# Two loops over attention heads, TensorE's and ScalarE's, written out head by head

## The chip, the cores and the metric

The kernel runs on one core of one Trainium2 chip. A core has several engines that each follow their own list of instructions: TensorE (matrix products; the profile calls it PE, and its weight loads PEld), VectorE (DVE), ScalarE (ACT), GpSimd (POOL) and SyncE (SP, which here starts the DMA transfers). They meet through semaphores: an instruction adds to a semaphore when it is done, and another engine waits until the semaphore has reached a value. The metric is the device time of one execution in microseconds (us); lower is better.

## The reference

x has 2048 tokens of 512 features. All products are wanted at about fp32 precision.

```python
x = x + 0.5 * ffn(layernorm(x))        # weights in 4-bit codes with block scales, MLP width 4096
x = x + attn(layernorm(x))
x = x + 0.5 * ffn(layernorm(x))

def attn(x):                           # 16 heads of 32 features, causal
    q, k, v = split(x @ w_qkv.T + b_qkv)
    scores = q @ k.T / sqrt(32) + causal_mask
    return (softmax(scores) @ v) @ w_out.T + b_out
```

## The kernel before

The kernel has four stages in a row, each a block in which every engine has its own program: the first feed-forward part, the projection to queries, keys and values, the attention, and the second feed-forward part. A stage begins when all engines have left the one before it.

**Feed-forward.** TensorE multiplies in groups of hidden features; after some groups written out, a loop `pe.Fori(1, NGROUP // 2 - 1)` runs two groups a round. The other engines have the same loop.

**Attention.** The 16 heads go one after the other. For a head, TensorE computes the scores twice. Once with queries as rows (`max_chunk`, L797), from which VectorE takes the row maxima (L820, L828); these become two further rows of the queries (`rows`, L808 and `store_rows`, L848 on ScalarE), so that the second scores already have the maximum taken off. That second time, keys are rows (`scores`, L1350; L1358 adds the causal mask); ScalarE takes the exponential of a tile (`exps`, L1551) into a ring of 12 tiles, and TensorE multiplies four tiles at a time with the values (`value_lane`, L1364) and with ones for the sums (`sum_lane`, L1370; GpSimd adds some tiles first, L1614). ScalarE copies a finished block of outputs from PSUM (`take_out`, L1559), four blocks to a head.

The order of work is written by hand. `head(hp, s)` works on head 3 hp + s: in each of its 40 slots it computes one tile of scores four slots ahead (`AHEAD`) and one chunk for the maxima of the head behind it. So the maxima of the next head are made during this one, and the score tiles run over the boundary between two heads: a boundary is no break in the work. Operands of a head lie in one of three buffers, `s % 3`, and so a round of three heads is the natural period. Heads 0 to 14 go through `head`; head 15 through `last_head`, between whose products the output projection starts.

Five programs hold this order. VectorE's, GpSimd's and SyncE's are Python loops (`for hp in range(...)`), so every instruction of every head stands in the program once. TensorE's (L1457) and ScalarE's (L1594) are loops of the chip: `Fori` puts the three heads of a round into the program once, `hp` is a register, and the end of a round is a branch back to its first instruction. Where a wait depends on `hp`, its value (such as `120 * hp + (SLOTS * s + u + 1)`) is worked out by the engine in a register operation ahead of the wait. There are five rounds, so four branches back; the fifth time the branch isn't taken.

Of the kernel before, what the change touches and what calls it, by code (L numbers as in the profile page):

```python
# [30 lines left out]
HEADS = 16  # L31
# [1149 lines left out]
def scaled_at(n):  # L1181
    b, k = STEPS[n]
    return QUARTERS * (SCALED.index(f"block {b}" if k == LATE_K else n) + 1)
# [71 lines left out]
def attention(nc, x, bank, o_heads, sums, inverses, w_out, b_out, heads, o):  # L1255
    with ExitStack() as ctx:
# [76 lines left out]
        def _(pe):  # L1333
# [4 lines left out]
            def scores(hp, s, u, first=False):  # L1338

                b, kt = TILES[u]  # L1340
                i = s % 3
                if u in FIRST_OF_BLOCK:
                    pe.wait_ge(heads.rows_ready, 12 * hp + (4 * s + RANK[b] + 1))
                    if s == 2 and u == 0:
                        pe.wait_ge(heads.constants_ready, 7)
                if not (first and u < SCORE_BANKS):
                    pe.wait_ge(probs_ready, 120 * hp + (SLOTS * s + u - SCORE_BANKS + 1))
                q0 = max(b * TB, kt * P)
                width = (b + 1) * TB - q0
                last = pe.matmul(score_bank_of(s, u)[:, 0:width], keys[i][0:ROWS, cols(kt, P)],  # L1350
                                 queries[i][0:ROWS, q0:q0 + width], start=True, stop=(kt < 4 * b),
                                 skip_group_check=True)
                if kt < 4 * b:
                    last.then_inc(scores_ready, 1)
# [54 lines left out]
            def head(hp, s):  # L1409
                for t in range(SLOTS):  # L1410
                    of, u = divmod(t + AHEAD, SLOTS)
                    scores(hp, s + of, u)
                    masks_of(s + of, u, False)
                    heads.max_chunk(pe, hp, s + 1, t)
                    if t in ROWS_AT:
                        heads.rows(pe, hp, s + (ROWS_AT[t] not in OWN_ROWS), ROWS_AT[t])
                    masks_of(s + of, u, True)
                    if t % BATCH == BATCH - 1:
                        meet_batch(hp, s, t // BATCH)
# [34 lines left out]

            for u in range(AHEAD):
                scores(0, 0, u, first=True)
            with pe.Fori(0, HEADS // 3) as hp:  # L1457
                for s in range(3):
                    head(hp, s)
            last_head(HEADS // 3)  # L1460
# [81 lines left out]
        @block.scalar  # L1542
        def _(act):
            def exps(hp, s, u, summed=True):
                b, kt = TILES[u]
                width = TB - max(0, kt * P - b * TB)
                i = u // BATCH - RING // BATCH
                if u % BATCH == 0 and summed and i % BATCHES in QUADS:
                    act.wait_ge(quad_steps, 54 * hp + 18 * (s + i // BATCHES + 1) + 3 * (QUADS.index(i % BATCHES) + 1))
                act.wait_ge(scores_ready, 120 * hp + (SLOTS * s + u + 1))  # L1550
                act.activation(probs[:, (SLOTS * s + u) % RING, 0:width],  # L1551
                               score_bank[(SLOTS * s + u) % SCORE_BANKS][:, 0:width],
                               ACT.Exp, scale=SM_SCALE).then_inc(probs_ready, 1)

            def take_out(hp, s, e):
                act.wait_ge(out_ready, 3 * NOUT * hp + (NOUT * s + e + 1))

                act.wait_ge(out_stored[e], 240 * hp + 80 * (s + 1))
                act.activation(heads_out[:, e, :, :], out_bank[:, 0:2 * P], ACT.Copy).then_inc(out_free, 1)  # L1559

            def take_outs(hp, s, t):
                if t in OUT_DONE:
                    take_out(hp, s, OUT_DONE.index(t))

            def head(hp, s):
                for t in range(SLOTS):
                    of, u = divmod(t + AHEAD, SLOTS)
                    exps(hp, s + of, u)
                    if t in ROWS_AT:
                        heads.store_rows(act, hp, s + (ROWS_AT[t] not in OWN_ROWS), ROWS_AT[t])  # L1570
                    if t % BATCH == BATCH - 1:
                        take_outs(hp, s, t)

            def high(n):
                act.wait_ge(o.scaled, scaled_at(n))
                act.activation(o.normed_high[:, n % UNITS, :], o.from_heads[:, n % UNITS, :], ACT.Copy)\
                   .then_inc(o.scaled_high, 1)

            def last_head(hp):
                for t in range(SLOTS):  # L1580
                    if t + AHEAD < SLOTS:
                        exps(hp, 0, t + AHEAD, summed=False)
                    if t in ROWS_AT and ROWS_AT[t] in OWN_ROWS:
                        heads.store_rows(act, hp, 0, ROWS_AT[t])
                    if t % BATCH == BATCH - 1:
                        for n in STEPS_AT.get(t // BATCH + 1, BEHIND[:3]):
                            high(n)
                        take_outs(hp, 0, t)
                for n in BEHIND[3:]:
                    high(n)  # L1590

            for u in range(AHEAD):
                exps(0, 0, u, summed=False)
            with act.Fori(0, HEADS // 3) as hp:  # L1594
                for s in range(3):
                    head(hp, s)
            act.wait_ge(o.wo_loaded, 16)
            act.activation(o.wo_high[:], o.wo[:], ACT.Copy).then_inc(o.wo_high_ready, 1)
            last_head(HEADS // 3)
# [125 lines left out]
```

## Time and profile before

| | |
|---|---|
| median of 3 runs | 2982.96 us (2982.94 to 2984.21) |
| the profiled execution's own time | 2983.2 us |
| its span, first to last instruction | 2981.4 us |
| TensorE busy | 2904.1 us, 97% of the span |
| ScalarE busy | 1052.5 us, 35% |
| granted TensorE clock, mean | 0.991 of full speed |
| attention, first score product to the last head's last copied block | 1267.55 to 1877.2 us |

Times in the profile are counted from the span's start. Busy time of an engine leaves out register operations, branches and waits. A granted clock of 1.00 is 2.4 GHz, 0.50 is 1.2 GHz.

### The profile page before, as it was taken

To read this page: it belongs to the slowest core of one execution; us is meant where nothing else is said; L and a number is where in the kernel's file an instruction comes from. 1 tells how busy PE (TensorE), PEld (TensorE's weight loads), DVE (VectorE), ACT (ScalarE), POOL (GpSimd) and SP (SyncE) were. 2 spreads that over 40 slices of the span, in tenths; PEclk is the share of its full clock that TensorE was granted. 3 is DMA by queue.
4 is the path that set the end of the run, shared out by engine and by line. 5 is a ranking of instruction groups with operands and counts; after the bars stand their busy time and mean duration, and the time that the engine had idled before them with its cause. 6 is when DMAs were issued, how large, how long until landed. Compare 5 with 4: busy or idle time off the path is not lost. (4 is left out here: it accounts for less than half of the span.)

```text
span 2981.4 us, 51041 instructions
## 1 busy us (share of the span) xinstructions
PE 2904.1 (97%) x19280; PEld 2342.2 (79%) x19280; DVE 1826.8 (61%) x3312; ACT 1052.5 (35%) x1825; POOL 1069.3 (36%) x745
## 2 busy tenths in 40 slices
PE   6999999999999999999999999899999999999999
PEld 5888888888888878777777776678888888888887
DVE  5656665565666544576777675675656665565654
ACT  4322222222222222266666664432222222222222
POOL 3322222222222224466666663342222222222221
PEclk9999999999999999999999999999999999999999
DMA  3001000000000015722322222100000000000001
GB/s 99 27 24 29 21 28 21 21 25 25 28 21 28 1 47 113 220 72 59 71 59 63 68 75 71 39 29 22 26 25 28 21 28 21 21 24 26 28 8 57
DMA packets 98586, 127.95 MB, mean 43 GB/s; under 512 B 43020, under 2 KB 51196, under 8 KB 95100
## 3 DMA queue, kind: packets, MB, share of 16 engines
q1 hardware_dynamic: 98428, 125.72, 15.3%
q8 instruction: 115, 1.88, 0.3%
q14 instruction: 43, 0.35, 0.0%
HBM read 96.34 MB, written 29.34 MB: 42 GB/s over the span
## 5 line engine op out<-in xcount | busy, mean ns | idle before, releaser
L59 PE MATMUL psum<-ffn_x_high,ffn_w_high 128*128 128x512 f32 x2048 | 801.6, 391 | 16.7 <-POOL ffn_x_low L212 9.5
L60 PE MATMUL psum<-ffn_x_low,ffn_w_high 128*128 128x512 f32 x2048 | 798.0, 390 | 0.0
L61 PE MATMUL psum<-ffn_x_high,ffn_w_low 128*128 128x512 f32 x2048 | 798.0, 390 | 0.0
L589 POOL TENSOR_TENSOR ffn_inner<-ffn_gelu,ffn_inner 128x512 fp32r<-128x512 f32 x256 | 345.6, 1350 | 1169.1 <-ACT ffn_inner L527 1169.1
L434 DVE SCALAR_TENSOR_TENSOR ffn_gelu<-ffn_gelu,psum 128x512 f32<-128x512 f32 x256 | 176.0, 687 | 604.1 <-ACT ffn_gelu L520 604.1
L59 PEld LDWEIGHTS psum<-ffn_x_high,ffn_w_high 128*128 128x128 f32 x2048 | 385.0, 188 | 105.4 <-POOL ffn_x_low L212 10.0
L61 PEld LDWEIGHTS psum<-ffn_x_high,ffn_w_low 128*128 128x128 f32 x2048 | 385.0, 188 | 80.1
L60 PEld LDWEIGHTS psum<-ffn_x_low,ffn_w_high 128*128 128x128 f32 x2048 | 385.2, 188 | 79.0
L59 PE MATMUL psum<-ffn_inner,ffn_w_high 128*128 128x512 f32 x1024 | 398.6, 389 | 0.2
L60 PE MATMUL psum<-ffn_inner,ffn_w_high 128*128 128x512 f32 x1024 | 398.4, 389 | 0.0
L61 PE MATMUL psum<-ffn_inner,ffn_w_low 128*128 128x512 f32 x1024 | 398.4, 389 | 0.0
L583 POOL TENSOR_TENSOR ffn_w_low<-ffn_weight,ffn_w_high 128x1024 fp32r<-128x1024 f32 x96 | 231.4, 2410 | 373.2 <-ACT ffn_w_high L513 373.2
L1551 ACT ACTIVATE probs<-psum 128x512 f32<-128x512 f32 (+3 forms) x640 | 297.9, 535 | 175.2 <-PE psum L1358 98.8
L520 ACT ACTIVATE ffn_gelu<-psum 128x512 f32<-128x512 f32 x256 | 153.0, 598 | 532.0 <-PE psum L61 532.0
L450 DVE SCALAR_TENSOR_TENSOR x<-psum,x 128x512 f32<-128x512 f32 x512 | 321.5, 683 | 20.5 <-PE psum L61 20.5
L820 DVE TENSOR_REDUCE chunk_max<-psum 128x1 f32<-128x512 f32 x384 | 249.6, 685 | 114.3 <-PE psum L797 114.3
L527 ACT ACTIVATE ffn_inner<-ffn_gelu 128x512 fp32r<-128x512 f32 x256 | 161.9, 633 | 381.1 <-DVE ffn_gelu L444 381.1
L438 DVE SCALAR_TENSOR_TENSOR ffn_gelu<-ffn_gelu,psum 128x512 f32<-128x512 f32 x256 | 176.3, 689 | 179.2 <-ACT ffn_gelu L522 179.2
L1350 PE MATMUL psum<-queries,keys 98*128 98x512 f32 (+3 forms) x640 | 258.5, 415 | 24.6 <-issue 13.4
L797 PE MATMUL psum<-keys,queries 96*128 96x512 f32 (+3 forms) x640 | 238.9, 381 | 1.1 <-DVE chunk_max L820 0.8
L1614 POOL TENSOR_TENSOR quads<-quads,probs 128x512 f32<-128x512 f32 x180 | 231.0, 1283 | 14.1
L522 ACT ACTIVATE ffn_gelu<-ffn_gelu 128x512 f32<-128x512 f32 x256 | 161.8, 632 | 204.1 <-DVE ffn_gelu L434 204.1
(120 smaller groups left out, 3520.5 us busy)
## 6 DMA issues: line engine op xcount, KB each, us to landing
ffn_words<-packed SPq DMA_DIRECT2D x96, 256.0 KB
ffn_word_scales<-scales SPq DMA_DIRECT2D x96, 256.0 KB
qk_parts<-parts SPq DMA_DIRECT2D x32, 512.0 KB, 3.9
queries<-qk_parts SPq DMA_DIRECT2D x48, 256.0 KB, 4.3
keys<-qk_parts SPq DMA_DIRECT2D x48, 256.0 KB, 6.2
x<-x_in SPq DMA_DIRECT2D x4, 1024.0 KB, 15.3
v_parts<-parts SPq DMA_DIRECT2D x16, 256.0 KB, 3.2
values<-v_parts SPq DMA_DIRECT2D x16, 256.0 KB, 7.0
```

What stands on the lines that cost most here:

```text
L59: pe.matmul(out, w_high, x_high, start=first, stop=False, skip_group_check=True)
L60: pe.matmul(out, w_high, x_low, start=False, stop=False, skip_group_check=True)
L61: return pe.matmul(out, w_low, x_high, start=False, stop=last, skip_group_check=True)
L438: dve.scalar_tensor_tensor(out=cubic[m], in0=square[m], scalar=1.0, in1=gate_bank[m], op0=ALU.add, op1=ALU.mult)\
L450: dve.scalar_tensor_tensor(out=x[:, k, cols(tb, TB)], in0=down_bank[k], scalar=FFN_BACK, in1=x[:, k, cols(tb, TB)], op0=ALU.mult, op1=ALU. ...
L583: pool.tensor_tensor(w_low[s][:, :, piece, :], weight[:, q % 2, :, :], f32(w_high[s][:, :, piece, :]), ALU.subtract).then_inc(w_low_ready, 1)
L589: pool.tensor_tensor(inner[:, tb % 2, m, 1, :], product[m], f32(inner[:, tb % 2, m, 0, :]), ALU.subtract)\
L797: last = pe.matmul(out[:, 0:width], self.queries[i][0:self.STACK, cols(qt, P)], self.keys[i][0:self.STACK, c * TB:c * TB + width], start=T ...
L820: dve.tensor_reduce(chunk_max, scores, AX.X, ALU.max).then_inc(self.max_taken, 1)
L1350: last = pe.matmul(score_bank_of(s, u)[:, 0:width], keys[i][0:ROWS, cols(kt, P)], queries[i][0:ROWS, q0:q0 + width], start=True, stop=(kt ...
L1551: act.activation(probs[:, (SLOTS * s + u) % RING, 0:width], score_bank[(SLOTS * s + u) % SCORE_BANKS][:, 0:width], ACT.Exp, scale=SM_SCALE ...
L1614: pool.tensor_tensor(total, total, tiles[j], ALU.add).then_inc(quad_steps, 1)
```

## The change

Two `Fori` become two Python loops. In the changed kernel `hp` is a plain number, TensorE and ScalarE have all 15 heads in their programs one after the other, each wait has a constant, and neither engine branches in this stage. The order and number of all products, activations, waits and transfers stay.

```diff
@@ block.tensor @@
             for u in range(AHEAD):
                 scores(0, 0, u, first=True)
-            with pe.Fori(0, HEADS // 3) as hp:
+            for hp in range(HEADS // 3):
                 for s in range(3):
                     head(hp, s)
             last_head(HEADS // 3)
@@ block.scalar @@
             for u in range(AHEAD):
                 exps(0, 0, u, summed=False)
-            with act.Fori(0, HEADS // 3) as hp:
+            for hp in range(HEADS // 3):
                 for s in range(3):
                     head(hp, s)
             act.wait_ge(o.wo_loaded, 16)
```

## Rows read from the trace of the kernel before

**Rows 1.** The page: its span, TensorE's busy time, the granted clock in 40 slices.

```profile
span 2981.4 us, 51041 instructions
...
PE 2904.1 (97%) x19280; PEld 2342.2 (79%) x19280; DVE 1826.8 (61%) x3312; ACT 1052.5 (35%) x1825; POOL 1069.3 (36%) x745
...
PEclk9999999999999999999999999999999999999999
```

**Rows 2.** Windows: start:end, length, busy (count) of PE, PEld, DVE, ACT, POOL; clock; DMA.

```profile
1306.32:1340.42 34.10, 33.83 (x513) 25.42 (x514) 25.65 (x84) 22.33 (x49) 23.09 (x19) 1.00 0.29 64
1340.42:1374.54 34.12, 33.80 (x512) 25.28 (x512) 25.66 (x84) 22.32 (x48) 22.99 (x19) 1.00 0.28 64
1374.54:1414.66 40.12, 36.84 (x513) 27.57 (x514) 25.89 (x84) 22.64 (x48) 22.97 (x19) 0.91 0.25 55
1414.66:1448.76 34.10, 33.83 (x513) 25.42 (x514) 25.65 (x84) 22.32 (x49) 23.09 (x19) 1.00 0.29 64
1448.76:1482.88 34.12, 33.80 (x512) 25.28 (x512) 25.66 (x84) 22.32 (x48) 22.99 (x19) 1.00 0.26 64
1482.88:1523.65 40.77, 37.01 (x513) 27.72 (x514) 25.88 (x84) 22.75 (x48) 22.98 (x19) 0.92 0.24 54
...
1591.90:1631.11 39.21, 35.59 (x513) 26.68 (x514) 25.88 (x84) 22.65 (x49) 23.02 (x19) 0.96 0.24 56
...
1699.35:1739.38 40.03, 36.53 (x513) 27.33 (x514) 25.88 (x84) 22.64 (x48) 23.00 (x19) 0.91 0.24 55
...
1773.47:1807.61 34.14, 33.88 (x513) 25.34 (x514) 26.76 (x86) 22.32 (x48) 21.43 (x17) 1.00 0.23 75
```

**Rows 3.** Timeline of TensorE about 1374 us: start, us, instructions, [idle before <-releaser].

```profile
1373.97 0.51 PE L1370 MATMUL psum<-probs,ones 128*32 128x128 f32 x11
1377.57 0.79 PE L1350 MATMUL psum<-queries,keys 98*128 98x512 f32 x1 [3.10 <-issue]
```

**Rows 4.** Timeline of ScalarE there, then of VectorE.

```profile
1378.40 0.60 ACT L1551 ACTIVATE probs<-psum 128x512 f32<-128x512 f32 x1 [3.48 <-PE psum L1350]
...
1378.83 0.69 DVE L820 TENSOR_REDUCE chunk_max<-psum 128x1 f32<-128x512 f32 x1 [4.46 <-PE psum L797]
```

**Rows 5.** Waits of TensorE, 1264 to 1808 us: total us, times, longest.

```profile
PE psum L1350 <- issue: 13.4, 4, 3.6
```

**Rows 6.** Windows again: behind an inner head boundary, then behind the four gaps.

```profile
1340.50:1346.50 6.00, 6.00 (x92) 4.77 (x91) 4.34 (x12) 5.01 (x10) 5.77 (x5) 1.00 0.37 88
1377.50:1383.50 6.00, 5.93 (x45) 4.57 (x46) 2.29 (x6) 2.97 (x5) 3.35 (x3) 0.50 0.81 185
...
1486.40:1493.00 6.60, 6.60 (x46) 5.21 (x47) 2.29 (x6) 3.07 (x6) 3.81 (x3) 0.50 0.92 211
...
1595.30:1598.80 3.50, 3.50 (x12) 2.83 (x12) 2.07 (x5) 2.05 (x4) 1.23 (x1) 0.52 0.53 134
...
1702.60:1708.00 5.40, 5.40 (x44) 4.31 (x44) 2.29 (x6) 2.97 (x5) 2.83 (x3) 0.50 0.69 172
```

**Rows 7.** Feed-forward loop, 320 to 970 us: windows.

```profile
320.00:970.00 650.00, 650.00 (x2870) 538.26 (x2869) 391.19 (x549) 179.73 (x268) 180.31 (x110) 1.00 0.08 24
```

**Rows 8.** DMA packets and queues from 400 to 900 us, in that loop.

```profile
DMA packets 6664, 12.49 MB, mean 25 GB/s; under 512 B 568, under 2 KB 568, under 8 KB 6664
...
q1 hardware_dynamic: 6664, 12.49, 7.9%
```

**Rows 9.** DMA queue q8: 1267 to 1374 us (round one), 1383 to 1482 us (round two).

```profile
q8 instruction: 12, 0.20, 0.9%
...
q8 instruction: 12, 0.20, 0.8%
```

**Rows 10.** Behind the loop: timeline of TensorE, of ScalarE, then a window.

```profile
1810.33 0.71 PE L1350 MATMUL psum<-queries,keys 98*128 98x512 f32 x1 [1.89 <-ACT probs L1551]
...
1807.89 1.90 ACT L1598 ACTIVATE wo_high<-wo 128x2048 fp32r<-128x2048 f32 x1
...
1810.50:1813.90 3.40, 3.40 (x53) 2.71 (x57) 3.40 (x1) 2.46 (x5) 3.40 (x1) 0.50 0.09 18
```

**Rows 11.** Windows of the second feed-forward part's start.

```profile
1899.30:1905.90 6.60, 4.49 (x56) 3.37 (x48) 4.37 (x7) 2.95 (x4) 2.36 (x1) 0.50 0.40 127
1947.10:1953.70 6.60, 6.13 (x13) 3.92 (x14) 5.15 (x4) 2.11 (x4) 3.89 (x4) 0.50 0.05 6
```

## The prediction, made before the changed kernel was run

> **What bounds the kernel now.** I read the page first: TensorE is busy 97% of the span and the granted clock is in the top tenth in every one of 40 slices [rows 1]. That names the engine, but an average over four stages can't say what five rounds of one loop cost, so the rest of the reading is in the attention stage.
>
> The second view is windows, one to a head. The edges are the starts of ScalarE's copy of a head's last block (L1559), an event that comes once at the same place of every head. The table falls into two kinds [rows 2]. Ten of the fourteen heads between the first and the last such copy take 34.1 us (34.09 to 34.14 us; five are shown). The four others take 40.12, 40.77, 39.21 and 40.03 us, and they are each third one: heads 3, 6, 9 and 12, the first heads of rounds two to five. Number of matmuls, VectorE's and ScalarE's work are the same in both kinds (512 or 513, 84, 48 or 49). In the short ones TensorE is busy 33.8 of 34.1 us at clock 1.00, so a head without disturbance is bound by TensorE. In the long ones the clock's mean is 0.91 to 0.96.
>
> The third view, the timeline, shows what stands at the start of a long head. TensorE ends head 2's last sums at about 1374.5 us and starts the next score product at 1377.57 us, idle for 3.10 us with "issue" named, that is, with no semaphore that the profile knows of [rows 3]. ScalarE and VectorE both wait for TensorE there, 3.48 and 4.46 us [rows 4]: they are not what it waits for. The view of waits counts four such idle times in the whole stage, 13.4 us together, 3.6 us the longest [rows 5]; the timeline has them at the starts of the four long heads, 3.10, 3.58, 3.44 and 3.31 us. All four lie where the `Fori` branches back.
>
> The fourth view, windows again, shows a second loss behind each. In the 6 us after an inner boundary TensorE does 92 matmuls at clock 1.00; in the 6 us after the first gap 45 at clock 0.50, 1.2 GHz instead of 2.4 [rows 6]. The three other falls come at the end of gaps of 3.3 to 3.6 us likewise. The clock is back some 3.5 to 7 us later.
>
> **The change part by part.**
>
> *The four branches back of TensorE go.* What takes their place is an inner boundary, for `head(hp, 2)` followed by `head(hp + 1, 0)` is the same code as `head(hp, 0)` followed by `head(hp, 1)` but for the indices of buffers and banks. So the price of a long head is its time less that of an undisturbed one [rows 2]: 40.12 - 34.12 = 6.00, 40.77 - 34.12 = 6.65, 39.21 - 34.12 = 5.09, 40.03 - 34.12 = 5.91, in sum 23.65 us. Of it 13.43 us are the gaps and the remaining 10.22 us the slow clock behind them. The second figure is borne out by [rows 6]: slow stretches of 6.0, 6.6, 3.5 and 5.4 us in which matmuls run at half speed cost half their length, 10.8 us.
>
> *Nothing else becomes the bound of a long head.* Its ScalarE work is 22.6 us, VectorE's 25.9, GpSimd's 23.0, all below 34.1 [rows 2]. The two heads behind each gap take 34.1 us one like the other, and so the 34.1 us don't live on a lead that the others gained in the gap. The stores and loads of SyncE are the same in each head; head 14, in which much more data moves besides, takes 34.14 us too.
>
> *Why the branch waits, and whether straight code does.* The feed-forward stage has loops too, and there TensorE is busy for 650.00 of 650 us [rows 7]. That stretch holds 2870 matmuls; by the code a round has two groups of 192 for gate and up and 96 for down, 576 in all or 130.5 us at this pace, so the window holds at least four branches back, and none costs a thing. In most of it, no packet of an instruction queue is seen: all 6664 packets are q1's [rows 8]. In attention a round is 1536 matmuls and as many weight loads, 3072 instructions against 1152, and q8 brings 12 packets in round one and 12 in round two, some 16 KB each [rows 9]. So a short body stays in the engine's reach, a long one is fetched anew in every round, and the branch is where the fetch is not yet on its way. The Trainium skill, page "Runtime: NRT & Kernel Launch", section "Instruction fetch mechanics", says that prefetch is purely sequential and that a taken branch out of the buffered pages waits for a DMA of the target; it gives TensorE's buffer as 2048 instructions, which lies between the two bodies. By that rule the trace agrees.
>
> *New code has to be fetched in place of repeated code.* Fetches stay about as many (12 a round). Round one of the loop is itself code that has not run before, and its second and third heads take 34.10 and 34.12 us, as those of round two [rows 2, 9]. So I take nothing for it.
>
> *ScalarE's branches go.* In the gap ScalarE waits for TensorE's product [rows 4], so its own branch is covered, by all but the last of 3.48 us; with TensorE's gap gone and its own loop left it could have come to light, at between nothing and those 3.5 us each. Both loops go together, and the term is nothing.
>
> *Register operations ahead of waits go,* on both engines. The views don't show them. From below nothing; from above the whole idle time of TensorE in an undisturbed head, 34.12 - 33.83 = 0.29 us, times 15, or 4.4 us [rows 2]. They run ahead while products are under way, so I take nothing.
>
> *What stays.* Behind the loop TensorE idles 1.89 us for an exponential that is queued behind ScalarE's 1.90 us copy of `wo`, and the clock falls to 0.50 for 3.4 us [rows 10]. Neither engine's order changes there. That fall costs 1.7 us, and two falls at the start of the second feed-forward part lie in stretches of 6.6 us [rows 11]. All come 23.65 us earlier. The four falls behind like gaps were of unlike length (3.5 to 6.6 us), so each of these may change by about 3.4 us of slow clock either way, worth 1.7 us each.
>
> The sum is made against the profiled execution: 2983.2 - 23.65 = 2959.6 us. That execution was 0.2 us over the median of the runs, so **2959.3 us** against 2982.96.
>
> **The rivals.**
>
> *The clock falls anyway.* The falls might come of the attention's mix of products, not of the gaps. For it: they come at nearly regular times, and one came behind only 1.89 us of idleness [rows 10]. Against it: each starts within about 1.5 us of a gap's end, and in the denser feed-forward stage the clock stays at 1.00 for 650 us [rows 7]. Then only the gaps go: 2983.0 - 13.4 = 2969.5 us.
>
> *The gap isn't the branch's.* If something else waits at a round's end and stays, the time is 2983 us. For it: the page names "issue" alone, and no row of the profile shows a branch. The Trainium skill, page "Advanced Engine Details and Errata", section "Control Flow Timing", gives about 108 ns to a compare-and-branch; by that price alone four branches would be worth 0.4 us and the sum would be 2982.5 us. Against it: nothing but the branch tells head 3 from head 4, and the gap is 3.1 to 3.6 us where a round ends and absent at ten inner boundaries.
>
> *Straight code starves.* This one is slower. If code never run before had to be waited for at each fetch, the 12 in each of four rounds would cost 48 times something. Below 23.65 / 48 = 0.49 us each the change still gains; above it loses, and at a full gap of 3.36 us each it would be 48 x 3.36 = 161 us, less 23.7: 3120 us. Against it stands round one, which is such code and shows no time above 34.12 us a head [rows 2, 9]; for it only that a longer program has more pages to miss.
>
> *The register operations did cost.* Then up to 4.4 us more: 2954.9 us.
>
> **How the numbers follow.** I give the forecast 0.86, the clock that falls anyway 0.05, a gap that isn't the branch's 0.03, starving 0.02, register operations 0.04. A change of over 0.2% is 6.0 us, about what a measurement of this kernel can tell from none. Forecast, clock and register cases are all faster than that (0.95), the gap that stays is no change (0.03), starving is slower (0.02). The range goes from 2959.3 down by 4.4 us for register operations and 1.7 us for a fall that vanishes, to 2953; and up by three falls that lengthen, 5.1 us, to 2965 with the rounding of the runs. It leaves out the clock case, the staying gap and starving, 1 in 10.
>
> **What would show each step.** In the profile after, windows from one last copied block to the next should all be 34.1 us, heads 3, 6, 9 and 12 among them, at clock 1.00. The waits of TensorE in the stage should have no "issue" of 3 us; busy time outside the stage should be as before. q8 should bring about 12 packets in the time of three heads still. If the heads at the old rounds' ends take 36.5 us or so, the gaps went and the slow clock stayed. If they take 40 us, the branch was not it. If all heads grow, the code starves; if all shrink below 34.0 us, the register operations counted.

## The result and the profile after

The changed kernel takes 2965.86 us (median of 4 runs, 2965.51 to 2967.59) against 2983.05 us: a ratio of 0.9943, 95% interval 0.9925 to 0.9960. It is faster, by 17.2 us and not by the 23.7 of the forecast, and lies 0.9 us above the range.

The page of the changed kernel, beside [rows 1]:

```profile
span 2964.2 us, 49479 instructions
...
PE 2899.2 (98%) x19280; PEld 2334.9 (79%) x19280; DVE 1831.5 (62%) x3312; ACT 1051.9 (35%) x1825; POOL 1069.9 (36%) x745
```

The same numbers of matmuls and activations stand on fewer instructions: the register operations are gone. Windows of the changed kernel, cut as in [rows 2]: heads 1, 2, 3, 4, 6, 9, 12 and 14, then the last head, then a stretch in it.

```profile
1306.14:1340.57 34.43, 34.05 (x513) 25.33 (x514) 25.79 (x84) 22.41 (x48) 23.06 (x19) 1.00 0.28 63
1340.57:1374.95 34.38, 34.01 (x513) 25.35 (x514) 25.81 (x84) 22.40 (x48) 23.01 (x19) 1.00 0.28 64
1374.95:1409.39 34.44, 34.08 (x513) 25.34 (x514) 25.81 (x84) 22.41 (x49) 23.05 (x19) 1.00 0.29 64
1409.39:1443.81 34.42, 34.05 (x513) 25.32 (x514) 25.79 (x84) 22.40 (x49) 23.05 (x19) 1.00 0.28 63
1478.18:1512.62 34.44, 34.08 (x513) 25.34 (x514) 25.81 (x84) 22.40 (x49) 23.05 (x19) 1.00 0.28 63
1581.42:1615.85 34.43, 34.07 (x513) 25.33 (x514) 25.81 (x84) 22.40 (x48) 23.04 (x19) 1.00 0.27 64
1684.65:1719.09 34.44, 34.08 (x513) 25.34 (x514) 25.81 (x84) 22.40 (x49) 23.05 (x19) 1.00 0.28 64
1753.51:1788.00 34.49, 34.12 (x513) 25.32 (x514) 26.92 (x86) 22.40 (x49) 21.39 (x17) 1.00 0.23 74
1788.00:1860.30 72.30, 65.68 (x733) 49.60 (x734) 37.79 (x49) 27.63 (x57) 23.73 (x15) 0.95 0.18 54
1796.50:1803.00 6.50, 6.01 (x24) 4.37 (x28) 2.67 (x2) 0.00 (x0) 2.12 (x2) 0.50 0.02 4
```

Two things are to be seen. Heads 3, 6, 9 and 12 are no longer than the others, at clock 1.00: gaps and slow clock are gone. But every head now takes 34.4 us where an undisturbed one took 34.1. So there is a loss that no row of before shows. The whole comes out of four stretches:

| stretch | before | after | difference |
|---|---|---|---|
| to the end of head 0 | 1306.32 | 1306.14 | -0.2 |
| heads 1 to 14 | 501.29 | 481.86 | -19.4 |
| last head | 69.55 | 72.30 | +2.8 |
| behind it, to the span's end | 1104.24 | 1103.90 | -0.3 |

The forecast for the second line was -23.65: 14 heads x 0.30 us = 4.2 us are missing from it. The waits of TensorE in that stage (1264 to 1788 us) answer to [rows 5]:

```profile
PE psum L1350 <- ACT probs L1551: 2.9, 16, 0.3
```

No "issue" is left; in its place TensorE waits in 16 places for an exponential. In the kernel before, the same view had one such wait, of 0.3 us, up to 1808 us. The 2.9 us are not the whole loss, for most of it counts as busy time: 34.05 us a head in place of 33.83, at the same number of products, which now start a little later behind one another. Where it starts is seen in two timelines, of the same place of head 4, at the tiles on the diagonal. Before (TensorE, then ScalarE):

```profile
1421.57 0.29 PE L1358 MATMUL psum<-key_mask_b,ident_b 128*128 128x128 bf16 x2
...
1421.98 0.28 PE L1350 MATMUL psum<-queries,keys 98*128 98x256 f32 x1
...
1422.49 0.33 PE L1350 MATMUL psum<-queries,keys 98*128 98x128 f32 x1
```

```profile
1421.84 0.98 ACT L1551 ACTIVATE probs<-psum 128x512 f32<-128x512 f32 x2 [1.59 <-PE psum L1358]
```

and after:

```profile
1416.33 0.29 PE L1358 MATMUL psum<-key_mask_b,ident_b 128*128 128x128 bf16 x2
...
1416.74 0.28 PE L1350 MATMUL psum<-queries,keys 98*128 98x256 f32 x1
...
1417.31 0.33 PE L1350 MATMUL psum<-queries,keys 98*128 98x128 f32 x1
```

```profile
1416.66 0.98 ACT L1551 ACTIVATE probs<-psum 128x512 f32<-128x512 f32 x2 [1.68 <-PE psum L1358]
```

From the mask product (L1358) to the exponential that waits for it, it was 0.27 us and is 0.33; and the score product that needs a bank which this exponential frees comes 0.57 us behind its forerunner in place of 0.51. So ScalarE starts 0.06 us late here, and TensorE has no slack for it. The views leave out waits and register operations, but the trace has records of them. Those of the exponential in the timelines above, before, then after (start in us, with the semaphores' names put in for their numbers):

```
1419.66 L1550 register operation, 35 ns [waits quad_steps]
1421.84 L1551 ACTIVATE probs<-psum [waits scores_ready]

1416.60 L1550 wait alone, 17 ns [waits scores_ready]
1416.66 L1551 ACTIVATE probs<-psum [waits quad_steps]
```

An exponential that opens a batch waits for two things: GpSimd's sums (`quad_steps`, long there) and the scores (`scores_ready`, the late one). In the loop the first wait sat on the register operation that works out the second's value, and the activation kept the late one. Without registers two waits are left for one activation. By the records it has only one of them, the sums; the scores' is an instruction of its own ahead of it, at 90 exponentials, six a head. The activation then starts only after that instruction has ended: 0.30 / 6 = 0.05 us a time in the mean. This is so far a theory; e1 to e4 test it.

### The profile page after: what moved, and what is told of

It is laid out like the page before. It is cut to its first block and busy times, and to the rows that moved or that the text cites. A ratio compares the mean times of both kernels' runs of the same rounds, so it can differ in the third digit from the quotient of the medians.

```text
span 2964.2 us, 49479 instructions
## 1 busy us (share of the span) xinstructions
PE 2899.2 (98%) x19280; PEld 2334.9 (79%) x19280; DVE 1831.5 (62%) x3312; ACT 1051.9 (35%) x1825; POOL 1069.9 (36%) x745
```

## The experiments

Ratios below are to the kernel before, run beside each on the same chip (medians of 2984.0 to 2984.5 us), with their 95% intervals.

**e1: TensorE's loop alone written out.**

```diff
-            with pe.Fori(0, HEADS // 3) as hp:
+            for hp in range(HEADS // 3):
```

> TensorE's loop written out, ScalarE's left as a loop. Theory A (the 0.3 us that each head is longer in the changed kernel come from ScalarE's program: where an exponential has two waits, the late one, on the scores, now stands in an instruction of its own ahead of it): no head behind head 0 takes more than 34.15 us, the gaps at the old round ends are gone, and the time is 2983 - 23.7 + about 2.7 for the slow clock that now falls into the last head's projections, 2962 us. Rival B (the 0.3 us come from TensorE's program, its waits split or its code fetched): all heads 34.4 us, 2966 us. Rival C (ScalarE's own branch back comes to light once TensorE's gap is gone): heads 3, 6, 9 and 12 take 35 to 38 us, 2965 to 2976 us.

Measured: 2961.21 us, 0.9922 (0.9908 to 0.9935). Two windows, heads 3 and 4:

```profile
1375.85:1410.01 34.16, 33.91 (x513) 25.34 (x514) 25.69 (x84) 22.32 (x48) 23.03 (x19) 1.00 0.28 64
1410.01:1444.15 34.14, 33.87 (x513) 25.34 (x514) 25.67 (x84) 22.34 (x49) 23.06 (x19) 1.00 0.28 64
```

The 0.3 us don't come from TensorE's program, and ScalarE's branch back costs nothing where it is alone: rivals B and C fall. The expected slow clock among the last head's projections did not come; that head takes 69.49 us. So it is partly luck that the time is so near the 2962 expected: the 2.7 us for that clock weren't lost, but head 0 ended at 1307.59 us in place of 1306.14, heads 1 to 14 kept about 0.5 us over the forecast, and the kernel before ran 1.4 us longer here too.

**e2: ScalarE's loop alone written out.**

```diff
-            with act.Fori(0, HEADS // 3) as hp:
+            for hp in range(HEADS // 3):
```

> ScalarE's loop written out, TensorE's left as a loop. Theory A: the ten inner heads take 34.4 us, the four at round ends 0.3 us more than before, about 40.3 us in the mean, with the gaps of 3.1 to 3.6 us as before; 14 x 0.3 = 4.2 us in sum, 2987 us. Rival B: inner heads 34.1 us, 2983 us.

Measured: 2986.90 us, 1.0011 (1.0002 to 1.0020). The waits of TensorE up to the end of head 14 have both losses side by side:

```profile
PE psum L1350 <- issue: 12.2, 4, 3.2
PE psum L1350 <- ACT probs L1551: 2.9, 16, 0.3
```

The inner heads take 34.29 to 34.40 us, those at round ends 40.12 to 40.42. Of the two edits that were one change, this half makes the kernel slower, by about 3 us.

**e3: both written out, the two waits exchanged.**

```diff
+                act.wait_ge(scores_ready, 120 * hp + (SLOTS * s + u + 1))
                 if u % BATCH == 0 and summed and i % BATCHES in QUADS:
                     act.wait_ge(quad_steps, ...)
-                act.wait_ge(scores_ready, 120 * hp + (SLOTS * s + u + 1))
```

> The changed kernel, both loops written out, with the order of two waits ahead of an exponential exchanged: first for the scores, then for GpSimd's sums. Theory A: the wait for the scores is then the one that stays on the exponential, and all heads take 34.1 us again; with the slow clock in the last head as it falls out, 2962 us (2960 to 2963). Rival B: heads stay at 34.4 us, 2966 us. Rival D (the 0.3 us are because the register operations are gone, whatever the waits' order): 34.4 us too.

Measured: 2960.75 us, 0.9920 (0.9907 to 0.9934). Head 3, head 4, and all of heads 1 to 14:

```profile
1374.96:1409.14 34.18, 33.92 (x513) 25.34 (x514) 25.67 (x84) 22.40 (x48) 23.03 (x19) 1.00 0.29 64
1409.14:1443.30 34.16, 33.90 (x513) 25.35 (x514) 25.69 (x84) 22.41 (x49) 23.09 (x19) 1.00 0.29 64
...
1306.65:1785.01 478.36, 474.73 (x7169) 354.84 (x7170) 360.78 (x1178) 313.74 (x673) 320.99 (x251) 1.00 0.29 69
```

With no register operation in either program, the order in which two waits are written is worth 481.86 - 478.36 = 3.5 us. Rival D falls, and the register operations themselves are worth nothing that shows.

**e4: the kernel before, the same two waits exchanged.**

> The kernel before, both loops kept, with the same two waits exchanged. Theory A: the wait for the scores then stands ahead of the exponential, on its own or on a register operation, and inner heads take at least the 0.3 us more that the changed kernel's do, 34.4 us or somewhat above, 2987 to 2990 us. Rival D: nothing changes, 34.1 us and 2983 us, since the register operations are there still.

Measured: 2988.75 us, 1.0014 (1.0005 to 1.0023). In the records the wait for the scores is now the one on the register operation. TensorE waits for exponentials 16 times, 3.2 us, as in the changed kernel, and a short head takes 34.34 to 34.41 us. So the loss can be put into the loops too. One row is enough, head 1:

```profile
1307.84:1342.21 34.37, 33.96 (x513) 25.34 (x514) 25.84 (x84) 22.39 (x48) 23.05 (x19) 1.00 0.28 64
```

**e5: one branch back in place of four.** From e3:

```diff
-            for hp in range(HEADS // 3):
-                for s in range(3):
-                    head(hp, s)
+            with pe.Fori(0, 2) as pair:
+                for s in range(6):
+                    head(pair * 2, s)
+            for s in range(3):
+                head(HEADS // 3 - 1, s)
```

> The kernel with the waits exchanged (2960.75 us), but TensorE's first twelve heads as a loop of two rounds of six heads, so one branch back in place of none (the kernel before has four). Theory: the gap and the slow clock belong to a taken branch with a long body, whatever its length: head 6 alone takes 39 to 41 us with an idle time of 3 to 3.6 us, and the time is about 2960.8 + 6 = 2966.8 us. Rival: the gap comes with the third head of a round or grows with the body: two gaps (2972 us), or one of 6 us (2970 us and more).

Measured: 2966.72 us, 0.9942 (0.9925 to 0.9958); 6.0 us over e3. Windows of heads 5, 6 and 7, and the timeline of TensorE:

```profile
1444.25:1478.38 34.13, 33.81 (x512) 25.29 (x512) 25.67 (x84) 22.40 (x48) 23.02 (x19) 1.00 0.28 64
1478.38:1518.38 40.00, 36.69 (x513) 27.40 (x514) 25.90 (x84) 22.72 (x48) 23.03 (x19) 0.91 0.24 55
1518.38:1552.52 34.14, 33.88 (x513) 25.42 (x514) 25.68 (x84) 22.41 (x48) 23.06 (x19) 1.00 0.28 65
```

```profile
1481.44 0.79 PE L1350 MATMUL psum<-queries,keys 98*128 98x512 f32 x1 [3.12 <-issue]
```

The price follows the taken branch: 5.9 us for one, and no more for a body twice as long.

**e6 and e7: idle times without a branch.** From e3, ahead of heads 3, 6, 9 and 12 a further copy on ScalarE (e6), or two (e7):

```diff
+                if hp >= 1:
+                    act.activation(o.wo_high[:], o.wo[:], ACT.Copy)
+                    act.activation(o.normed_high[:, 0:KT, :], o.wo[:], ACT.Copy)   # e7 only
+                else:
+                    act.wait_ge(o.wo_loaded, 16)
                 for s in range(3):
                     head(hp, s)
-            act.wait_ge(o.wo_loaded, 16)
```

> The kernel with the waits exchanged, no branch, and ahead of heads 3, 6, 9 and 12 one further copy of the output weights on ScalarE, 1.9 us, whose result is what stands there anyway; TensorE then idles for about 1.9 us at each old round end. Theory (idleness makes the clock fall, not the branch): the clock is seen at 0.50 behind each, and each costs 1.9 us and 1.7 to 3.4 more: 2975 to 2982 us. Rival (the clock falls from the branch or of itself, or 1.9 us are too short where the work around them is dense): no fall, 4 x 1.9 = 7.6 us, 2968 us.

> The same with a second copy (into a buffer that nothing reads until the last head), so that TensorE idles for about 3.8 us at each old round end, a little more than at the branches. Theory: four falls as in the kernel before; each place costs 3.8 + 2.6 us, 2986 us. Rival: no fall, 4 x 3.8 = 15.2 us, 2976 us.

Measured: 2977.27 us, 0.9977 (0.9967 to 0.9986), and 2991.30 us, 1.0024 (1.0015 to 1.0034). Both times hold a mistake of the edit: the wait for the weights now stands ahead of head 0, where TensorE waits 8.1 us for it, and head 0 ends at 1315.89 us in e6 in place of 1306.65. The windows of single heads are free of that. In e6, head 3 and what follows its idle time of 1.19 us:

```profile
1384.15:1419.76 35.61, 34.17 (x513) 25.26 (x514) 25.76 (x84) 24.08 (x50) 23.06 (x19) 1.00 0.27 62
1386.90:1393.00 6.10, 6.10 (x93) 4.71 (x94) 2.97 (x10) 4.22 (x9) 4.86 (x4) 1.00 0.85 200
```

In e7, head 3, what follows its idle time, and the idle time:

```profile
1383.93:1422.73 38.80, 35.56 (x513) 26.19 (x514) 25.76 (x84) 25.89 (x51) 23.05 (x19) 0.96 0.25 57
1388.50:1391.40 2.90, 2.90 (x38) 2.25 (x38) 0.29 (x3) 1.96 (x4) 2.30 (x2) 0.50 1.08 246
```

```profile
1388.45 0.80 PE L1350 MATMUL psum<-queries,keys 98*128 98x512 f32 x1 [2.99 <-ACT probs L1551]
```

TensorE idled less than I had reckoned, for it has six products in hand when the copies start: 1.19 us behind one copy, 2.99 behind two. After 1.19 us the clock stays at 1.00 in this trace, four times of four, and a head is 1.5 us longer. That is one execution: it took 2975.30 us at a mean clock of 0.994, and one more of the ten was like it. The other eight took 2976.45 to 2978.41 us at 0.991 or 0.992, so they had slow clock somewhere that this trace has not; they have no trace, and a fall behind 1.19 us can't be excluded in them. After 2.99 us the clock is at 0.50, four times of four, where TensorE neither branches nor waits for code but for ScalarE: heads 3, 6, 9 and 12 take 38.80, 39.73, 41.84 and 39.90 us, 23.7 us over four undisturbed ones, of which 12.0 are idle time. That is nearly the sum of the four branches. So the idleness makes the clock fall. The rival of the prediction, a clock that falls anyway, is out: e3 has none between heads 1 and 14.

**e9: a long body in the feed-forward part.** The kernel before, and

```diff
-            with pe.Fori(1, NGROUP // 2 - 1) as gg:
-                group(gg, 0, False)
-                group(gg, 1, False)
+            with pe.Fori(0, (NGROUP // 2 - 2) // 2) as r:
+                for half in range(2):
+                    group(r * 2 + (half + 1), 0, False)
+                    group(r * 2 + (half + 1), 1, False)
```

> The kernel before, both attention loops kept, with TensorE's feed-forward loop made of three rounds of four groups in place of six rounds of two: a body of 2304 matmuls and weight loads in place of 1152, and two branches back in each feed-forward part in place of five. Theory (a body that is longer than what the engine keeps is fetched anew and the branch waits for it): two gaps of 3 to 3.6 us in each part, each with a slow clock behind it, 4 x 6 = 24 us, 3007 us. Rival (attention's gap has another cause, such as the reads of a register or the score tiles that run over the boundary): no gap, 2983 us.

Measured: 2985.38 us, 1.0005 (0.9995 to 1.0015): no difference, the rival's number. But the profile shows half of the theory. Windows from 320 to 970 us, then DMA from 400 to 900 us, beside [rows 7, 8], and q8 from 449 to 459 us, about a branch back:

```profile
320.00:970.00 650.00, 650.00 (x2870) 538.21 (x2869) 391.37 (x549) 179.67 (x268) 180.10 (x110) 1.00 0.08 25
```

```profile
q1 hardware_dynamic: 6629, 12.42, 8.2%
q8 instruction: 21, 0.34, 0.3%
...
q8 instruction: 3, 0.05, 2.2%
```

With the short body no packet was fetched in these 500 us, with the long one 21 are, three of them in the 10 us about the branch. So the long body is fetched anew. And TensorE never stops. The trace's records of the branches, which the views don't list, say 3.4 us for each of the two in this stretch, 3.8 and 3.9 us for the two in the second feed-forward part (where TensorE is busy throughout as well), 3.65 to 4.14 us for the four in attention of the kernel before, and 0.21 to 0.23 us for the short body: it is a long branch here too. What differs, as I read it, is what TensorE still has to do. Here it has products in hand, issued ahead and waiting for nothing, and works through the fetch.

**e10: the round cut behind score products.** From e3, TensorE's loop again, four rounds, cut between the four slots' products and the batch of value products:

```diff
+            for t in range(BATCH):
+                slot(0, 0, t)
+            with pe.Fori(0, HEADS // 3 - 1) as hp:
                 for s in range(3):
-                    head(hp, s)
+                    head(hp, s, before=BATCH * (s == 0))
+                for t in range(BATCH):
+                    slot(hp, 3, t)
```

> The kernel with the waits exchanged (2960.75 us), TensorE again with a loop of three heads, but four rounds (the last three heads and head 15 written out), so three branches back; and the round is cut four slots later, ahead of a batch of value products: so the last things issued ahead of the branch are seven score products of 512 columns and a short one, about 1.8 us of work, and not value products of 27 ns each. Theory (the branch takes about 3.6 us and what has been issued ahead of it goes on meanwhile; the idle time is what the issued work doesn't cover): three idle times of 1.2 to 2.3 us, now ahead of value products or the products behind them, and with that little idleness no or fewer slow stretches; 2960.8 + 3 x 1.8 = 2966 us, up to 2971 with the clock. Rival (the gap is 3.1 to 3.6 us wherever the branch stands): three gaps of that size with the slow clock, 2960.8 + 3 x 5.9 = 2978.5 us.

Measured: 2981.70 us, 0.9993 (0.9983 to 1.0003). Wrong: three idle times of 11.8 us together, the longest 4.33, with the slow clock behind.

```profile
1377.16 0.40 PE L808 MATMUL psum<-ident_r,max_parts 128*2 128x128 f32 x4
1381.89 1.94 PE L1364 MATMUL psum<-probs,values 128*32 128x128 f32 x32 [4.33 <-issue]
```

The heads with a cut take 40.13, 40.48 and 40.03 us, as in the kernel before. By the trace's records the branch was issued at 1376.99 us, when about half a microsecond of the eight products was left, and it took 4.64 us (the third 3.51). I had taken it that products which wait for ScalarE would be issued well ahead; here they weren't. Why they weren't is open, and so no run shows that the branch in attention can be covered; that products in hand cover one rests on e9.

**e8: the output weights copied earlier.** From e3, ScalarE's copy of `wo` in quarters, ahead of two output copies each in heads 13 and 14, where it waits for TensorE. The copy behind the loop goes, and GpSimd waits for all four quarters (neither is shown):

```diff
                     if t % BATCH == BATCH - 1:
+                        if t in OUT_DONE and 3 * hp + s in (HEADS - 3, HEADS - 2) and OUT_DONE.index(t) < 2:
+                            k = 2 * (3 * hp + s - (HEADS - 3)) + OUT_DONE.index(t)
+                            if k == 0:
+                                act.wait_ge(o.wo_loaded, 16)
+                            act.activation(o.wo_high[:, k, :], o.wo[:, k, :], ACT.Copy).then_inc(o.wo_high_ready, 1)
                         take_outs(hp, s, t)
```

> The kernel with the waits exchanged, and ScalarE's 1.9 us copy of the output weights taken from the start of the last head and done as four quarter copies ahead of output copies in heads 13 and 14, where ScalarE waits for TensorE; GpSimd's subtraction follows head 14's sums, as it did, but starts earlier. Theory (what the last head loses is TensorE's 1.9 us wait behind that copy, the 0.4 to 2.0 us wait for GpSimd that follows, and the slow clock that these bring): both waits gone and no slow stretch there, last head 66 to 67.5 us in place of 69.5, 2957 to 2959 us. Rival (the last head is bound elsewhere, by ScalarE or the transfers): 69 us still, 2960.5 us or more.

Measured: 2955.97 us, 0.9907 (0.9890 to 0.9923), the lowest median of all, 28.4 us under the kernel before beside it and 9.9 under the changed one. The last head and TensorE's waits in it:

```profile
1784.42:1850.10 65.68, 62.74 (x733) 47.68 (x734) 32.34 (x49) 25.93 (x56) 17.90 (x14) 1.00 0.20 59
```

```profile
PE psum L1350 <- ACT probs L1551: 2.9, 9, 0.5
```

**e8b: TensorE's waits too.** From e8, in `scores` the wait on `probs_ready` is put ahead of the one on `rows_ready`.

> The same with the two waits ahead of TensorE's first score product of a block exchanged too, so that the one for the exponentials stays on the weight load. If late waits that stand alone cost TensorE as well, heads take 34.12 in place of 34.15 us and the time is 0.5 us less; if not, no difference. Both are near what the rounds can tell; the head times decide.

Measured: 2957.01 us, 0.9910 (0.9894 to 0.9927), inner heads 34.14 to 34.18 us: no difference. The exchange touches four products a head, and no row shows that the moved wait is the late one there; so it shows only that the order of these two is worth nothing on TensorE.

## Why the prediction was wrong

*Four branches back: right.* Heads 3, 6, 9 and 12 became like the others, and where the waits are in order (e1, e3) heads 1 to 14 take 478.1 and 478.4 us, 22.9 to 23.2 less than 501.29; the forecast was 23.65. The split into gap and slow clock holds as well: the gap follows the branch (e5), the clock the idleness (e7). That the gap isn't the branch's, that the clock falls anyway and that straight code starves are refuted by e5, by e3 and e7, and by the windows after; q8 brings 12 packets in the changed kernel too (1375 to 1478 us).

*ScalarE's branches at nothing: right*, and for more than the cover that I named: with TensorE's gap gone (e1) no head shows one; the trace's records give it 0.045 us.

*The register operations: this step failed.* "From below nothing; from above the whole idle time of TensorE in an undisturbed head." I bounded it as a gain only. (The 0.29 us take the length from one row and the busy time from another; within a row they are 0.27 or 0.32 us, so 4.1 to 4.8 us in 15 heads, which changes nothing.) The operation also carried one of two waits. Without it the late wait moved into an instruction of its own, at 0.05 us each, six a head, and heads 1 to 14 lost 3.5 us by e3, 3.2 by e2 (504.46 us against 501.29). I could have known of the two waits from the code (L1549 and L1550); no row of before shows what they cost, but that ScalarE and TensorE wait for each other at the diagonal tiles with little slack was to be seen.

*What stays: right in kind, short in size.* I allowed each fall 1.7 us. The last head lost 2.75 us, for the fall came later and lasted longer. In both kernels a chain of ScalarE's copy (`wo_high`) and GpSimd's subtractions (`wo_low`, `normed_low`) lets the projections begin 9.0 us after the last copied block. In the kernel before, the slow stretch lay ahead of that, in work that had to wait anyway, and TensorE then waited 0.42 us for GpSimd. In the changed one TensorE was fast there, waited 2.01 us, and was slow in the projections behind: the first twelve products took 5.4 us in place of 3.0. Before, then after:

```profile
1816.57 0.50 PE L59 MATMUL psum<-normed_high,wo_high 128*128 128x512 f32 x1 [0.42 <-POOL normed_low L1629]
...
1796.98 0.80 PE L59 MATMUL psum<-normed_high,wo_high 128*128 128x512 f32 x1 [2.01 <-POOL normed_low L1629]
```

With the copy out of the way (e8) the last head has clock 1.00 and takes 65.68 us. Why the first idle time of 1.9 us, alike in both, brought a fall once and once not, no run settles. It isn't the written-out code by itself: in e1 and e3 TensorE's program is written out too and the last head takes 69.49 and 69.52 us, and in e10, with a loop, 72.27.

Together: 23.65 forecast, less 3.5 for the wait, less 0.7 that even e3 keeps over the forecast in heads 1 to 14 (478.36 against 501.29 - 23.65 = 477.64; 0.05 us a head, cause open), less 2.75 for the last head, plus 0.5 in the first and last line of the table, is 17.2 us. Either of the two losses alone, 3.5 or 2.75, would have left the time inside the range.

What the Trainium skill says of fetches on the page "Runtime: NRT & Kernel Launch", section "Instruction fetch mechanics", agrees with the packets of e9: a body of 2304 matmuls and weight loads, over the 2048 instructions that the page gives for TensorE, is fetched anew, one of 1152 isn't. Its sentence that such a branch "forces a DMA fetch of the target page before execution can continue" holds for what TensorE issues, not for what it has in hand: in e9 it stayed busy.

## What to carry to other kernels

A loop of the chip costs where its body is longer than what the engine keeps and what is issued ahead doesn't cover the fetch: look at the engine's idle time at round ends and at the instruction queue's packets, and count the slow clock behind the gap with it. When registers, or anything that can carry a wait, are taken out of a program, look where each of the waits ends up, and write first the one that comes last: here that order was worth 3.5 us, a fifth of what the change gained. And where engines take turns closely, half of a change can be a loss: try each half alone.

## What the runs showed of the hardware

- A taken branch to code that has to be fetched takes 3.4 to 4.6 us of TensorE's issuing by the trace's records; in the feed-forward part TensorE lost nothing by it (650.00 of 650 us busy), in attention all but 0.55 us (3.65 us for a gap of 3.10). To code still at hand it takes 0.2 us, ScalarE's 0.045 us.
- In the profiled executions an idle TensorE of 1.19 us left the clock at 1.00 four times of four, one of 2.99 us brought it to 0.50 four times of four, and one of 1.9 us did either.
- Of two waits with constants written ahead of an activation, the first written stays on it and the second becomes an instruction of its own (with registers, the first goes to a register operation and the second stays); the late wait off the activation costs ScalarE about 0.05 us. On TensorE's weight loads no cost was seen, at four a head.
